# The head of a fused attention block in four chunks instead of two, and a copy of scores moved in front of an exponential in two tiles

## The chip, the cores and the metric

One core of one Trainium2 chip runs the whole program. The metric is the device time of one execution in microseconds (us), and lower is better. The engines are TensorE (PE; its weight loads are shown as PEld), VectorE (DVE), ScalarE (ACT), GpSimd (POOL) and SyncE (SP), which issues all the DMAs of this kernel.

## The reference, cut to what matters

The block has three residual layers: cross-attention over a context of 2048 rows, self-attention with relative positions, and a gated attention layer. Batch is 4, there are 128 queries, the width is 512 and there are 16 heads of 32. The change touches the first layer only:

```python
x = x + cross_attention(layernorm(x), ctx, ctx, Wq, bq, Wk, bk, Wv, bv, Wo, bo)
# in cross_attention
q = (query @ Wq + bq).reshape(Bq, Sq, H, DK)
k = (key @ Wk + bk).reshape(Bq, Sk, H, DK)
v = (value @ Wv + bv).reshape(Bq, Sk, H, DK)
scores = jnp.einsum('bqhd,bkhd->hbqk', q, k) / np.sqrt(DK)
attn = jax.nn.softmax(scores.reshape(H * Bq, Sq, Sk), axis=0)   # over the 64 (head, batch) pairs
out = jnp.einsum('hbqk,bkhd->bqhd', attn, v)
```

The softmax runs over the 64 pairs of head and batch and not over the keys, so each block of 128 keys can be finished by itself.

## The kernel before, in words

**Tiles.** The first layer walks over the context in T = 16 tiles t of 128 keys (times 4 batches, so 512 columns). For each tile TensorE projects the keys K (four banks i, `project_k`, L466) and the values V (four batches b, `project_v`, L489), multiplies queries with keys (four groups of heads w, `score`, L510) and, two tiles later in program order, probabilities with values (`attend`, L533). ScalarE copies K, V and the scores out of PSUM (`k_copy` L1027, `v_copy` L1037, `s_copy` L1045) and takes the exponentials in eight pieces p (`exp`, L1061). VectorE takes the maximum over the 64 pairs (L1540), subtracts it (L1562), sums the exponentials (L1569), inverts (L1582) and scales two pieces of the eight (L1610); GpSimd subtracts it from two pieces (L1378), scales the other six (L1384), and computes the low parts of the context (L1357).

**Two parts.** Each operand of a projection is split into a high part (a rounded copy, by ScalarE or GpSimd) and a low part (a subtraction, by VectorE or GpSimd). Each product has three terms, in the order of `PARTS`: high times high, high data times low weight, low data times high weight.

**Order.** Nothing schedules this program: every engine runs its instructions in the order in which its block of the code issues them, and semaphores (`wait_ge`, `then_inc`) tie the engines. An instruction that waits holds everything behind it on its engine. The SyncE block issues the loads in order; their data goes out on one queue in that order.

**The head.** Before the first tile SyncE loads the first half of the key weight `Wk1` and of the context (512 KB each), the four pieces of x (256 KB each), the second halves, and then `Wq1`, `Wv1` and the small tables. TensorE keeps itself busy with 14 products of the identity (`keep_warm`, L552), and then runs `first_keys(k, n)` for half k and term n (L566), with the transposes of the normalised x (L371) between them, then the queries (`query`, L587), a small product for the relative positions (L607), which waits for `tab_mul`, and the first scores. ScalarE splits the halves (L1069, L1074), takes the square roots of the layer norm (L1004), copies the transposed x (`query_hi`, L1078) and half of the query weight (L1097). VectorE makes the low parts (L1484, L1489), the layer norm (L1457 to L1466), the low part of the transposed x (L1506) and that of the whole query weight (L1509).

**In a tile.** ScalarE's list for tile t begins with k_copy(t, 0), v_copy(t-1, 1) and a context split, then exp(t-1, 0), s_copy(t, 0), exp(t-1, 1), k_copy(t, 1), exp(t-1, 2), v_copy(t-1, 2) and exp(t-1, 3). TensorE waits for these copies in several places. The two that matter here are:

```python
                else:
                    pe.wait_ge(s["s_evac"], min(2 * (C * t + 3 + b) - 1, 2 * C * T))
```

in `project_v` (L486), by which V(t-1, 2) waits for the first of the two copies of s_copy(t, 0), since that bank held those scores; and `pe.wait_ge(s["kv_evac"], k_step(t, w) + 1)` in `score` (L503), by which the scores of group w wait for k_copy(t, w).

## Time and profile before

| | us |
|---|---|
| three runs | 720.54, 720.43, 720.11 |
| median | 720.43 |
| the profiled execution, its own time | 720.23 |
| its span, first to last instruction | 718.4 |
| PE busy in the span | 701.2 (98%) |
| DVE busy | 627.3 (87%) |
| POOL busy | 502.6 (70%) |
| ACT busy | 487.8 (68%) |

A busy share says how full an engine is, not whether it sets the end. For that one follows the chain of waits back from the last instruction, and looks in the timeline at what each engine waited for. The head (up to the first scores) ends at 26.6 us, and the sixteen tiles follow. The granted TensorE clock reads 1.00 in all slices of the span.

### The profile page before, as it was taken

The page shows a single profiled execution, that of the slowest core. Times are in us where ns is not written, and L with a number is a line of the kernel's source. Part 1 is how long each engine was busy: PE and PEld are TensorE (multiplying, and loading weights), DVE is VectorE, ACT ScalarE, POOL GpSimd, SP SyncE. Part 2 cuts the span into 40 slices and gives each one's busy share as a digit, 9 for nine tenths or more (in the row PEclk, how much of TensorE's full clock was granted, in tenths as well). Part 3 has the DMA queues.
Part 4 walks back from the last instruction along what each step waited for, and adds up shares of the span by engine and source line. Part 5 has one row for each costly group of instructions (what it writes and reads, how often), then busy time and mean ns, then how long its engine had stood idle before and what let it go on. Part 6 is the DMA issues. An engine that isn't in the chain of part 4 may idle for free.

```text
span 718.4 us, 17265 instructions
## 1 busy us (share of the span) xinstructions
PE 701.2 (98%) x7511; PEld 561.6 (78%) x7511; DVE 627.3 (87%) x514; ACT 487.8 (68%) x696; POOL 502.6 (70%) x284
## 2 busy tenths in 40 slices
PE   8999999999999999999999999999999999999988
PEld 7777788888888888888888888887668667878876
DVE  6678999999999999999999999999987458977785
ACT  5578668686776867777686776868643446735682
POOL 1564979999999999999999999996894010054400
PEclk9999999999999999999999999999999999999999
DMA  9411020101101010110101011010003899631101
GB/s 332 147 48 34 26 61 2 59 2 59 56 6 61 1 60 1 60 59 2 61 1 61 20 42 60 2 59 2 1 5 113 284 393 385 254 104 59 60 2 58
DMA packets 15675, 55.74 MB, mean 78 GB/s; under 512 B 1648, under 2 KB 2160, under 8 KB 12272
## 3 DMA queue, kind: packets, MB, share of 16 engines
q1 hardware_dynamic: 15600, 54.64, 21.0%
q8 instruction: 59, 0.97, 0.5%
q14 instruction: 16, 0.13, 0.1%
HBM read 43.16 MB, written 11.47 MB: 76 GB/s over the span
## 4 chain that ended last, share of the span: by engine, by line
PE 74%; DVE 12%; DMA 6%; ACT 4%; issue 2%; SPq 1%; POOL 0%; DVEq 0%; POOLq 0%; ACTq 0%
PE ps L466 22%; PE ps L489 21%; PE ps L510 9%; PE ps L533 8%; DMA rel_scratch<-blocks 5%; DVE extra L1540 2%; PE ps L444 2%; PE ps L855 2%; PE ps L380 2%; DVE extra L1569 2%; PE ps L587 2%; PE ps L837 1%; PE ps L388 1%; DVE ps L1569 1%; PE ps L399 1%
## 5 line engine op out<-in xcount | busy, mean ns | idle before, releaser
L1384 POOL TENSOR_TENSOR s_buf<-s_buf,r_all 128x1024 f32<-128x1024 f32 x92 | 195.1, 2159 | 1.0 <-DVE r_all L1582 1.0
L1045 ACT COPY s_buf<-ps 128x1024 f32<-128x1024 f32 x128 | 123.2, 1016 | 30.4 <-PE ps L510 30.4
L1061 ACT ACTIVATE s_buf<-s_buf 128x1024 f32<-128x1024 f32 x128 | 134.2, 1064 | 8.2 <-DVE s_buf L1562 8.2
L1540 DVE TENSOR_REDUCE extra<-s_buf 128x128 f32<-128x2048 f32 x48 | 109.3, 2277 | 4.6 <-ACT s_buf L1045 4.6
L1562 DVE TENSOR_TENSOR s_buf<-s_buf,ps 128x2048 f32<-128x2048 f32 x48 | 106.9, 2282 | 0.5
L1351 POOL TENSOR_TENSOR v_buf<-v_buf,extra 128x512 f32<-128x512 f32 x64 | 81.0, 1301 | 8.2 <-ACT v_buf L1037 8.2
L1037 ACT COPY v_buf<-ps 128x512 f32<-128x512 f32 x64 | 37.6, 587 | 65.2 <-PE ps L489 64.4
L1569 DVE TENSOR_REDUCE ps<-s_buf 128x128 f32<-128x4096 f32 (+1 forms) x16 | 67.6, 4227 | 15.2 <-ACT s_buf L1061 15.1
L1362 POOL TENSOR_TENSOR w_lo<-raw,w_hi 128x2048 fp32r<-128x2048 f32 x5 | 23.1, 4618 | 82.1 <-ACT w_hi L1012 82.1
L510 PEld LDWEIGHTS ps<-q_t,k_t 32*128 32x128 f32 x2048 | 63.0, 186 | 18.9 <-issue 17.5
L510 PE MATMUL ps<-q_t,k_t 32*128 32x128 f32 x2048 | 75.1, 283 | 0.4 <-ACT k_t L1027 0.2
L1569 DVE TENSOR_REDUCE extra<-s_buf 128x128 f32<-128x2048 f32 x32 | 72.8, 2276 | 1.1 <-ACT s_buf L1061 1.1
L1378 POOL TENSOR_TENSOR s_buf<-s_buf,m_all 128x2048 f32<-128x2048 f32 x16 | 66.0, 4124 | 6.9 <-DVE m_all L1555 6.9
L533 PEld LDWEIGHTS ps<-s_buf,v_buf 128*32 128x32 f32 x2048 | 56.3, 108 | 14.7 <-issue 14.3
L533 PE MATMUL ps<-s_buf,v_buf 128*32 128x128 f32 x2048 | 66.0, 278 | 1.3 <-DVE s_buf L1610 1.3
L1357 POOL TENSOR_TENSOR odd_lo<-extra,odd_hi 128x512 fp32r<-128x512 f32 x32 | 41.1, 1300 | 21.9 <-ACT odd_hi L1020 21.8
L1027 ACT ACTIVATE k_t<-ps,cols 128x512 f32<-128x512 f32 x64 | 43.8, 690 | 8.1 <-PE ps L466 3.9
L1357 POOL TENSOR_TENSOR x_lo<-raw,x_hi 128x512 fp32r<-128x512 f32 x28 | 35.9, 1295 | 12.9 <-ACT x_hi L1020 12.7
L1540 DVE TENSOR_REDUCE ps<-s_buf 128x128 f32<-128x2048 f32 x16 | 36.7, 2296 | 6.0 <-ACT s_buf L1045 4.6
L1610 DVE TENSOR_TENSOR s_buf<-s_buf,ps 128x2048 f32<-128x2048 f32 x18 | 41.0, 2285 | 0.5
L1391 POOL TENSOR_TENSOR acc<-acc,late 128x512 f32<-128x512 f32 x26 | 34.0, 1307 | 7.6 <-ACT late L1053 7.6
L466 PE MATMUL ps<-odd_hi,w_hi 128*128 128x512 f32 x128 | 36.3, 405 | 0.0
(265 smaller groups left out, 1476.6 us busy)
## 6 DMA issues: line engine op xcount, KB each, us to landing
rel_scratch<-blocks SPq DMA_DIRECT2D x16, 636.0 KB, 10.8
s_buf<-rel_scratch SPq DMA_DIRECT2D x7, 1210.0 KB, 9.6
extra<-in_ctxT SPq DMA_DIRECT2D x8, 1024.0 KB, 4.9
raw<-in_ctxT SPq DMA_DIRECT2D x7, 1024.0 KB, 4.9
raw<-in_Wq SPq DMA_DIRECT2D x2, 1024.0 KB, 7.2
raw<-in_Wv SPq DMA_DIRECT2D x2, 1024.0 KB, 4.9
extra<-in_EvRel SPq DMA_DIRECT2D x1, 2048.0 KB, 12.5
extra<-rel_scratch SPq DMA_DIRECT2D x1, 1210.0 KB, 10.1
```

Of the source, the lines that this page charges most:

```text
L466: last = mm(ps[:, k_bank(t, i), :], w_parts[v][:, 0, n % C, i * P:(i + 1) * P], ctx_parts[t % 2][u][:, n % C, :], start=n == 0, stop=n == ...
L489: last = mm(ps[:, v_bank(t, b), :], ctx_parts[t % 2][u][:, n % C, b * P:(b + 1) * P], w_parts[v][:, 1, n % C, :], start=n == 0, stop=n == ...
L510: last = mm(pair, k_t[rows, w, keys], q_t[rows, w, keys], start=True, stop=True, skip_group_check=True)
L533: last = mm(ps[j * HD:(j + 1) * HD, bank, b * P:(b + 1) * P], v_of(t)[:, b, h * HD:(h + 1) * HD], probs[:, j, b // 2, :, b % 2], start=b = ...
L1045: copy(piece(t, 2 * w + u).rearrange("p e (u n) -> p (e u) n", u=2), ps[:, 2 * u:2 * u + 2, :]).then_inc(s["s_evac"], 1)
L1061: nc.scalar.activation(piece(t, p), piece(t, p), ACT.Exp).then_inc(s["exp_done"], 1)
L1351: pool.tensor_tensor(v, v, bv_all, ALU.add).then_inc(s["v_ready"], 1)
L1357: pool.tensor_tensor(lo[:, :, rows], raw_of(t)[:, :, rows], hi[:, :, rows], ALU.subtract).then_inc(s["ctx_lo"], 1)
L1384: pool.tensor_tensor(part, part, spread(r_all, 4), ALU.mult).then_inc(s["attn_pool"], 1)
L1540: nc.vector.tensor_reduce(m_ps if k == 0 else m_next[:, k % 2, :], over_pairs(t, 2 * k, 2), AX.XY, ALU.max).then_inc(s["max_done"], 1)
L1562: tt(part, part, m_wide.broadcast_to([P, 8, P, 2]), ALU.subtract).then_inc(s["sub_dve"], 1)
L1569: nc.vector.tensor_reduce(r_ps if k == 0 else z_next[:, k % 2, :], over_pairs(t, p, n), AX.XY, ALU.add).then_inc(s["sum_done"], 1)
```

## The change

SyncE now loads key weight and context in four chunks each (256 KB, one chunk c of 128 rows of the contraction), in turn, and all eight in front of x; the rest follows in the old order. TensorE runs 8 products of the identity instead of 14, and then the keys chunk by chunk with all three terms, only the last term of the last chunk between the transposes. ScalarE and VectorE split chunk by chunk, and the layer norm comes after that. The low part of the query weight is made half by GpSimd and half by VectorE, and VectorE's half comes after the table for the positions; the queries run their terms in the order 0, 2, 1. One copy of K goes between two copies of the transposed x. In tiles 1 and 2 ScalarE runs s_copy(t, 0) and k_copy(t, 1) in front of exp(t-1, 0). The semaphores for the chunks are ones used again later, so that later waits rise by 16.

```diff
+        FIRST_WK = ("wk_in", "wkb_ev_in", "head_rq_in_0", "head_rq_in_1")
+        FIRST_CTX = ("ctx_in_0", "ctxb_b3_in", "head_rq_in_2", "head_rq_in_3")
...
-            first, rest = slice(0, C // 2), slice(C // 2, C)
-            load(wk_raw[:, first], a["Wk1"][:, first], "wk_in")
-            load(raw[:, first], a["ctxT"][0][:, first], "ctx_in_0")
+            for c in range(C):
+                load(wk_raw[:, c], a["Wk1"][:, c], FIRST_WK[c])
+                load(raw[:, c], a["ctxT"][0][:, c], FIRST_CTX[c])
             for b in range(B):
                 load(x_res[:, b, :], a["x"][b], f"x_in_{b}")
-            load(wk_raw[:, rest], a["Wk1"][:, rest], "wkb_ev_in")
-            load(raw[:, rest], a["ctxT"][0][:, rest], "ctxb_b3_in")
...
             pe.wait_ge(s["ident_done"], 2)
-            keep_warm(3, 14)
-            for n in range(3):
-                first_keys(0, n)
+            keep_warm(3, 8)
+            for c in range(C - 1):
+                first_keys(c, range(3))
+            first_keys(C - 1, range(2))
             transposes(y_ln0, 0, 0)
             transposes(y_ln0, 0, 1)
-            first_keys(1, 0)
+            first_keys(C - 1, (2,))
             transposes(y_ln0, 0, 2)
             transposes(y_ln0, 0, 3)
-            first_keys(1, 1)
-            first_keys(1, 2)
             query(0, 0)
+            query(0, 2)
             pe.wait_ge(s["tab_mul"], 1)
...
             query(0, 1)
-            query(0, 2)
...
                 query(w + 1, 0)
                 score(0, w)
+                query(w + 1, 2)
                 query(w + 1, 1)
-                query(w + 1, 2)
...
-            first_weight_hi(0, "wk_in")
-            first_ctx_hi(0, "ctx_in_0")
-            ln_std(0, 0)
-            ln_std(0, 1)
-            first_weight_hi(1, "wkb_ev_in")
-            ln_std(0, 2)
-            first_ctx_hi(1, "ctxb_b3_in")
-            ln_std(0, 3)
+            for c in range(C):
+                first_hi(c)
+            for b in range(B):
+                ln_std(0, b)
             query_hi(0)
-            query_hi(1)
             act.wait_ge(s["wq_in"], 16)
             copy(wq_hi[:, 0:2], wq_raw[:, 0:2]).then_inc(s["wq_split"], 1)
+            query_hi(1)
+            act.wait_ge(s["cols_in"], 16)
+            act.wait_ge(s["ln_done"], B)
+            k_copy(0, 0)
             query_hi(2)
             query_hi(3)
...
-                exp(t - 1, 0)
+                if t > 2:
+                    exp(t - 1, 0)
                 s_copy(t, 0)
 
+                if t <= 2:
+                    k_copy(t, 1)
+                    exp(t - 1, 0)
                 exp(t - 1, 1)
-                k_copy(t, 1)
+                if t > 2:
+                    k_copy(t, 1)
...
             pool.tensor_copy(wq_hi[:, 2:4], wq_raw[:, 2:4]).then_inc(s["wq_split"], 1)
+            pool.wait_ge(s["wq_split"], 2)
+            pool.tensor_tensor(wq_lo[:, 2:4], wq_raw[:, 2:4], wq_hi[:, 2:4], ALU.subtract).then_inc(s["wq_split"], 1)
             pool.wait_ge(s["wv_in"], 16)
...
+            for c in range(C):
+                first_lo(c)
             moments0(0)
...
             normalised(0, 3)
-            first_weight_lo(1)
-            first_ctx_lo(1)
...
-            dve.wait_ge(s["wq_split"], 2)
-            tt(wq_lo[:], wq_raw, wq_hi[:], ALU.subtract).then_inc(s["wq_split"], 1)
             nc.vector.memset(r_all[:], 1.0).then_inc(s["ones_done"], 1)
             dve.wait_ge(s["tab_in"], 16)
...
+            dve.wait_ge(s["wq_split"], 2)
+            tt(wq_lo[:, 0:2], wq_raw[:, 0:2], wq_hi[:, 0:2], ALU.subtract).then_inc(s["wq_split"], 1)
```

The new `first_hi(c)` copies chunk c of the weight and then of the context once each has landed, `first_lo(c)` subtracts both, and `first_keys(c, terms)` runs four products (one per bank) for each term of chunk c.

TensorE at the head, from the keys to the first scores, before (`x_hi`, `x_lo` are the context, `w_hi`, `w_lo` the key weight, `xq` and `wq` the queries' side):

```order
L566 MATMUL ps<-x_hi,w_hi 128x512 x8
L566 MATMUL ps<-x_hi,w_lo 128x512 x8
L566 MATMUL ps<-x_lo,w_hi 128x512 x8
L371 MATMUL ps<-ident,v_buf 128x128 x8
L566 MATMUL ps<-x_hi,w_hi 128x512 x8
L371 MATMUL ps<-ident,v_buf 128x128 x8
L566 MATMUL ps<-x_hi,w_lo 128x512 x8
L566 MATMUL ps<-x_lo,w_hi 128x512 x8
L587 MATMUL ps<-xq_hi,wq_hi 128x512 x4
L607 MATMUL ps<-tab,r_all 128x255
L587 MATMUL ps<-xq_hi,wq_lo 128x512 x4
L587 MATMUL ps<-xq_lo,wq_hi 128x512 x4
```

And now, from the last chunk of the keys on (three chunks of twelve products stand in front of these rows):

```order
L566 MATMUL ps<-x_hi,w_hi 128x512 x4
L566 MATMUL ps<-x_hi,w_lo 128x512 x4
L371 MATMUL ps<-ident,v_buf 128x128 x8
L566 MATMUL ps<-x_lo,w_hi 128x512 x4
L371 MATMUL ps<-ident,v_buf 128x128 x8
L587 MATMUL ps<-xq_hi,wq_hi 128x512 x4
L587 MATMUL ps<-xq_lo,wq_hi 128x512 x4
L607 MATMUL ps<-tab,r_all 128x255
L587 MATMUL ps<-xq_hi,wq_lo 128x512 x4
```

The count of key products is 48 in both, but 44 of them now stand in front of the first transpose, where 24 stood, and the last term of query group 0 is the one with the low weight.

ScalarE between the layer norm's roots and the first copy of queries, before:

```order
L1078 CAST xq_hi<-ps 128x4x128 x2
L1097 CAST wq_hi<-s_buf 128x1024
L1078 CAST xq_hi<-ps 128x4x128 x2
L1027 ACTIVATE k_t<-ps,cols 128x512 x4
L1083 ACTIVATE q_t<-ps,q_add 128x512
```

and now (the line numbers are those of the changed file):

```order
L1073 CAST xq_hi<-ps 128x4x128
L1087 CAST wq_hi<-s_buf 128x1024
L1073 CAST xq_hi<-ps 128x4x128
L1026 ACTIVATE k_t<-ps,cols 128x512
L1073 CAST xq_hi<-ps 128x4x128 x2
L1026 ACTIVATE k_t<-ps,cols 128x512 x3
L1078 ACTIVATE q_t<-ps,q_add 128x512
```

The four copies of the transposed x are spread further, around the copy of the query weight and one of K.

ScalarE in tile 1, before:

```order
L1020 CAST x_hi<-raw 128x4x128
L1061 ACT_TABLE_LOAD
L1061 ACTIVATE s_buf<-s_buf 128x1024
L1045 COPY s_buf<-ps 128x1024 x2
L1061 ACTIVATE s_buf<-s_buf 128x1024
L1027 ACTIVATE k_t<-ps,cols 128x512
L1061 ACTIVATE s_buf<-s_buf 128x1024
L1037 COPY v_buf<-ps 128x512
```

and now:

```order
L1019 CAST x_hi<-raw 128x4x128
L1044 COPY s_buf<-ps 128x1024 x2
L1026 ACTIVATE k_t<-ps,cols 128x512
L1060 ACT_TABLE_LOAD
L1060 ACTIVATE s_buf<-s_buf 128x1024 x3
L1036 COPY v_buf<-ps 128x512
```

The load of the exponential's table and three exponentials now stand behind the copy of K.

## Rows read from the trace of the kernel before

**Rows 1.** The page, busy time of each engine.
```profile
PE 701.2 (98%) x7511; PEld 561.6 (78%) x7511; DVE 627.3 (87%) x514; ACT 487.8 (68%) x696; POOL 502.6 (70%) x284
```

**Rows 2.** Chain of waits, 0 to 100 us: start, length, what.
```profile
56.63 4.43 DVE ps L1569
```

**Rows 3.** Timeline of PE, head: start, length, line, operands, count, idle before.
```profile
8.08 2.08 PE L566 MATMUL ps<-x_hi,w_hi 128*128 128x512 f32 x8 [1.58 <-ACT x_hi L1074]
...
13.62 1.03 PE L371 MATMUL ps<-ident,v_buf 128*128 128x128 f32 x8
...
20.87 1.07 PE L587 MATMUL ps<-xq_hi,wq_hi 128*128 128x512 f32 x4
22.96 0.69 PE L607 MATMUL ps<-tab,r_all 32*128 32x255 f32 x2 [1.02 <-DVE tab L1512]
23.58 1.21 PE L587 MATMUL ps<-xq_hi,wq_lo 128*128 128x512 f32 x4
24.63 1.09 PE L587 MATMUL ps<-xq_lo,wq_hi 128*128 128x512 f32 x4
```

**Rows 4.** Timeline of ACT, head.
```profile
5.01 1.05 ACT L1069 CAST w_hi<-s_buf 128x1024 fp32r<-128x1024 f32 x1 [2.79 <-DMA s_buf<-in_Wk]
...
6.79 1.14 ACT L1074 CAST x_hi<-raw 128x512 fp32r<-128x512 f32 x2 [0.73 <-DMA raw<-in_ctxT]
...
14.26 1.07 ACT L1078 CAST xq_hi<-ps 128x512 fp32r<-128x512 f32 x2 [0.68 <-PE ps L371]
...
15.22 1.06 ACT L1097 CAST wq_hi<-s_buf 128x1024 fp32r<-128x1024 f32 x1
...
25.82 0.69 ACT L1083 ACTIVATE q_t<-ps,q_add 128x512 f32<-128x512 f32 x1 [3.60 <-PE ps L587]
```

**Rows 5.** Timeline of DVE, head.
```profile
8.66 0.69 DVE L1457 BATCH_NORM_STATS2 stats<-x_res 128x6 f32<-128x512 f32 x1
...
13.98 0.55 DVE L1466 TENSOR_SCALAR v_buf<-x_res,mean_var,rstd 128x512 f32<-128x512 f32 x1
...
20.02 2.47 DVE L1509 TENSOR_TENSOR wq_lo<-s_buf,wq_hi 128x2048 fp32r<-128x2048 f32 x1
```

**Rows 6.** Windows of the first 12 us: stretch, busy per engine, PEclk, DMA share, GB/s.
```profile
4.00:6.00 2.00, 2.00 (x17) 2.00 (x16) 0.00 (x0) 0.99 (x1) 0.00 (x0) 1.00 0.97 296
6.00:8.00 2.00, 0.49 (x5) 0.30 (x3) 1.78 (x2) 1.20 (x3) 0.00 (x0) 1.00 1.03 387
```

**Rows 7.** Windows of the identity products alone (L552): PE, PEld, PEclk, DMA share, GB/s.
```profile
3.00:4.00 1.00, 1.00 (x6) 1.00 (x6) 1.00 0.88 254
...
5.00:6.00 1.00, 1.00 (x12) 1.00 (x11) 1.00 0.96 309
```

**Rows 8.** Timeline of ACT, tiles 1 and 3.
```profile
47.87 0.62 ACT L1020 CAST x_hi<-raw 128x512 fp32r<-128x512 f32 x1
48.51 1.28 ACT L1061 ACT_TABLE_LOAD   x1
49.81 1.06 ACT L1061 ACTIVATE s_buf<-s_buf 128x1024 f32<-128x1024 f32 x1
50.78 1.90 ACT L1045 COPY s_buf<-ps 128x1024 f32<-128x1024 f32 x2
...
109.90 1.06 ACT L1061 ACTIVATE s_buf<-s_buf 128x1024 f32<-128x1024 f32 x1 [0.37 <-DVE s_buf L1562]
110.86 1.91 ACT L1045 COPY s_buf<-ps 128x1024 f32<-128x1024 f32 x2
```

**Rows 9.** Timeline of PE, tiles 1 to 3.
```profile
50.33 1.07 PE L466 MATMUL ps<-odd_lo,w_hi 128*128 128x512 f32 x4
...
54.36 1.17 PE L510 MATMUL ps<-q_t,k_t 32*128 32x128 f32 x32 [0.24 <-ACT k_t L1027]
...
81.87 1.20 PE L489 MATMUL ps<-w_hi,odd_hi 128*128 128x512 f32 x4 [1.10 <-ACT s_buf L1045]
...
113.17 1.07 PE L489 MATMUL ps<-w_hi,x_hi 128*128 128x512 f32 x4
```

More of the change, by code:

```diff
@@ L325, in rel_load @@
                 dst = rk_part(u) if kind else rq_part(u)
-                load(dst[:, :, 0:RUN], rows, f"rk_in_{u}" if kind else f"rq_in_{u}")
+                load(dst[:, :, 0:RUN], rows, f"rk_in_{u}" if kind else f"head_rq_in_{u}")
             for n in range(4):
@@ L552, in keep_warm, with first_keys @@
                     mm(ps[:, bank, 0:P], ident[:], ident[:], start=True, stop=True, skip_group_check=True)
-            def first_keys(k, n):
-                u, v = PARTS[n]
-                if n == 0:
-                    pe.wait_ge(s["wkv_hi"], k + 1)
-                    pe.wait_ge(s["ctx_hi"], 2 * k + 2)
-                elif v:
-                    pe.wait_ge(s["wkv_lo"], k + 1)
-                else:
-                    pe.wait_ge(s["ctx_lo"], 2 * k + 2)
-                for hg in range(C):
-                    for c in (2 * k, 2 * k + 1):
+            def first_keys(c, terms):
+                for n in terms:
+                    u, v = PARTS[n]
+                    if n == 0:
+                        pe.wait_ge(s["wkv_hi"], c + 1)
+                        pe.wait_ge(s["ctx_hi"], c + 1)
+                    elif v:
+                        pe.wait_ge(s["wkv_lo"], c + 1)
+                    else:
+                        pe.wait_ge(s["ctx_lo"], c + 1)
+                    for hg in range(C):
                         last = mm(ps[:, k_bank(0, hg), :], w_parts[v][:, 0, c, hg * P:(hg + 1) * P], x_parts[u][:, c, :],
-                                  start=(k, n, c) == (0, 0, 0), stop=(k, n, c) == (1, 2, C - 1), skip_group_check=True)
-                    if (k, n) == (1, 2):
-                        last.then_inc(s["kv_psum"], 1)
+                                  start=(c, n) == (0, 0), stop=(c, n) == (C - 1, 2), skip_group_check=True)
+                        if (c, n) == (C - 1, 2):
+                            last.then_inc(s["kv_psum"], 1)
             def query(hg, n):
@@ L587, in query @@
                     last = mm(ps[:, q_bank(hg), :], (wq_hi, wq_lo)[v][:, c, hg * P:(hg + 1) * P], (xq_hi, xq_lo)[u][:, c, :],
-                              start=n == 0 and c == 0, stop=n == 2 and c == C - 1, skip_group_check=True)
-                if n == 2:
+                              start=n == 0 and c == 0, stop=n == 1 and c == C - 1, skip_group_check=True)
+                if n == 1:
                     last.then_inc(s["q_psum"], 1)
             pe.wait_ge(s["ident_done"], 2)
-            keep_warm(3, 14)
-            for n in range(3):
-                first_keys(0, n)
+            keep_warm(3, 8)
+            for c in range(C - 1):
+                first_keys(c, range(3))
+            first_keys(C - 1, range(2))
             transposes(y_ln0, 0, 0)
             transposes(y_ln0, 0, 1)
-            first_keys(1, 0)
+            first_keys(C - 1, (2,))
             transposes(y_ln0, 0, 2)
             transposes(y_ln0, 0, 3)
-            first_keys(1, 1)
-            first_keys(1, 2)
             query(0, 0)
+            query(0, 2)
             pe.wait_ge(s["tab_mul"], 1)
@@ L1065, in _, with first_hi @@
             act.wait_ge(s["eps_done"], 2)
-            def first_weight_hi(k, name):
-                part = slice(2 * k, 2 * k + 2)
-                act.wait_ge(s[name], 16)
-                copy(w_hi[:, 0, part], wk_raw[:, part]).then_inc(s["wkv_hi"], 1)
-            def first_ctx_hi(k, name):
-                act.wait_ge(s[name], 16)
-                for c in (2 * k, 2 * k + 1):
-                    copy(x_hi[:, c, :], raw[:, c, :]).then_inc(s["ctx_hi"], 1)
+            def first_hi(c):
+                act.wait_ge(s[FIRST_WK[c]], 16)
+                copy(w_hi[:, 0, c], wk_raw[:, c]).then_inc(s["wkv_hi"], 1)
+                act.wait_ge(s[FIRST_CTX[c]], 16)
+                copy(x_hi[:, c, :], raw[:, c, :]).then_inc(s["ctx_hi"], 1)
             def query_hi(b):
@@ L1107, in _ @@
             ctx_split(1, 1)
-            act.wait_ge(s["wkv_lo"], 3)
+            act.wait_ge(s["wkv_lo"], C + 1)
             for w in range(1, C):
@@ L1479, in moments0, with first_lo @@
                 moments(0, b)
-            def first_weight_lo(k):
-                part = slice(2 * k, 2 * k + 2)
-                dve.wait_ge(s["wkv_hi"], k + 1)
-                tt(w_lo[:, 0, part], wk_raw[:, part], w_hi[:, 0, part], ALU.subtract).then_inc(s["wkv_lo"], 1)
-            def first_ctx_lo(k):
-                for c in (2 * k, 2 * k + 1):
-                    dve.wait_ge(s["ctx_hi"], c + 1)
-                    tt(x_lo[:, c, :], raw[:, c, :], x_hi[:, c, :], ALU.subtract).then_inc(s["ctx_lo"], 1)
-            first_weight_lo(0)
-            first_ctx_lo(0)
+            def first_lo(c):
+                dve.wait_ge(s["wkv_hi"], c + 1)
+                tt(w_lo[:, 0, c], wk_raw[:, c], w_hi[:, 0, c], ALU.subtract).then_inc(s["wkv_lo"], 1)
+                dve.wait_ge(s["ctx_hi"], c + 1)
+                tt(x_lo[:, c, :], raw[:, c, :], x_hi[:, c, :], ALU.subtract).then_inc(s["ctx_lo"], 1)
+            for c in range(C):
+                first_lo(c)
             moments0(0)
```

18 lines of the change are left out of this document (8 added, 10 removed).

## The prediction

> **What bounds the kernel now.** I read the page first. TensorE is busy for 701.2 of 718.4 us and VectorE for 627.3 [rows 1], so the kernel is near TensorE's own length, and only time in which TensorE waits, or works on a later schedule than it could, can be won. The chain of waits was next. It begins with the loads and the layer norm, runs along VectorE from 56.63 us [rows 2], and changes to TensorE at 81.87 us, where TensorE had stood 1.10 us for ScalarE's copy of scores [rows 9]. From there to the end of the tiles it stays on TensorE. So there are two limits in turn: VectorE's chain in tiles 0 to 2 and TensorE's from tile 2 on, and a gain must pass through both. The timelines of the head then show where the start is lost: TensorE's first key product at 8.08 us, after 1.58 us without work, and 1.02 us lost at 22.96 us to VectorE's table, which stood behind the 2.47 us subtraction of the whole query weight [rows 3, 5]. All sums below are on the profiled execution, 720.23 us with its 1.8 us around the span; the median of the runs is 0.2 us above it.
>
> **The head, step by step.** Loads: the queue gives its data in order. The first 512 KB were there at 5.01 us, 1 MB at 6.79 us, when ScalarE took them up [rows 4]. The first chunk pair is now exactly the first 512 KB, so ScalarE can copy the context chunk at 5.0 us; one of the two copies of 1.14 us is 0.6 us, and TensorE began 0.15 us after the last one (6.79 + 1.14 = 7.93, then 8.08). First key product: 5.0 + 0.6 + 0.15 = 5.75, I take 5.8 us instead of 8.08. The later pairs come every 1.3 to 1.8 us (512 KB at 387 and at 296 GB/s, [rows 6]) and TensorE needs 2.8 us for each, so only the first pair counts.
>
> TensorE: 24 key products took 13.62 - 8.08 = 5.54 us, 0.23 each [rows 3]. Now 44 stand in front of the transposes: 5.8 + 44 x 0.23 = 15.9 us. The layer norm took 13.98 + 0.55 - 8.66 = 5.9 us of VectorE [rows 5]; it now comes after the last low part of a context chunk (2 MB at 9.7 us by the rates above, two copies and subtractions behind it: 11.1 us) and ends at 17.0 us, its second quarter near 15. TensorE asks for the second quarter at 16.3 and for the last at 17.7, so moving it costs nothing, with 0.7 us of cover.
>
> ScalarE becomes the bound here. Its first copy of transposed x began 0.64 us after the transposes (14.26 against 13.62, [rows 3, 4]): 16.55 us. Then come, less the overlap of neighbours, 0.5 (x), 1.0 (query weight, 1.06 in the row), 0.5 (x), 0.6 (one K copy, priced by the same form at 25.82 us), 0.5 and the last 0.6 [rows 4]: 20.2 us. Query group 0 can start at 20.35 us, 0.5 us earlier than its 20.87, while TensorE waits some 1.9 us. But then little is lost: 0.92 for the first term, 0.92 for the second, which needs the low part of x (VectorE, 20.8 us, in time), the product for positions at 22.2 (its table is now in front of the weight's subtraction and ready at 21.3), 0.62 to the last term at 22.8 us, which needs both halves of the low weight. GpSimd's half is done near 20.4 (from 18.05, at twice VectorE's length at most 2.5); VectorE's takes half of 2.47 and ends at 22.55, so 0.25 us of cover. Before, the last group began at 24.63 and the copy of queries at 25.82, 1.19 later, and a group behind the product for positions is 0.13 longer (1.05 against 0.92): the copy starts at 24.1 us. **Head: 25.82 - 24.1 = -1.7 us.** The value weight's low part (the form of 2.47 us, behind the product for positions) ends near 25.7 us, and the first scores (0.7 for the copy, 1.2 for the products) near 26.0, so it stays hidden. What follows up to tile 1 is TensorE without a wait and moves as a block.
>
> **Tile 1, ScalarE** (times in the old frame, to be moved by the head). The context split ends at 48.49. Before, table load, exponential, scores copy and K copy followed without a gap [rows 8]. Now the scores copy runs 48.51 to 50.41 and the K copy waits for its product, which ends at 50.33 + 1.07 = 51.40 [rows 9]. So ScalarE stands 1.0 us, and the table load, which starts only when the copy has ended, and all that is behind it come later by 1.0 plus some 0.2 of overlap lost: the fourth exponential by 1.25 us. VectorE's sum at 56.63 waits for it and begins the chain [rows 2], so **VectorE's chain is 1.25 us later**. In return TensorE's 0.24 us at 54.36 and, in tile 2, the 1.10 us at 81.87 go [rows 9], because the scores copy no longer stands behind an exponential; about 0.8 us come back as waits for ScalarE's later K copy and GpSimd's later scaled pieces. TensorE enters tile 3 some 0.6 us ahead.
>
> **Tile 3** keeps the old order. There the exponential at 109.90 waits for VectorE, and the scores copy at 110.86 is behind it; TensorE took the bank at 113.17 [rows 8, 9]. With VectorE's chain 1.25 us late the exponential starts at 111.15, the copy at 112.1, its first half ends at 113.1, and TensorE goes on at 113.15 with 0.13 us for a restart, although it was ready at 112.6. The stall removed in tile 2 is back in tile 3. **Tiles: +0.1 us** against before. From then on VectorE, with 627 us of work against TensorE's 701 [rows 1], makes its lateness up, and the order no longer matters.
>
> **Sum:** 720.23 - 1.7 + 0.1 = **718.6 us**. What is not in the trace: the cost of 2 KB rows for the first chunks. The bounds for the first pair are 5.0 us, when as many bytes were there before, and 6.8 us, when twice as many were [rows 4]; earlier than 5.0 it can't be, as ScalarE stood waiting for those bytes. I take 5.0, since the bytes and their place in the queue are the same; the upper end would eat the whole 1.7. The Trainium skill ("DMA: Bandwidth & Descriptors", Measured) speaks against it: it wants at least 1 MiB in a DMA for 75% of peak and gives 138 GB/s for 64 KB and 341 for 1 MB. At an estimated 250 GB/s by that page the pairs would come every 2.1 us, still under TensorE's 2.8 us, and the sum would lose only what the first pair is late.
>
> **The rivals.**
> (a) *Both stalls go.* If ScalarE's standing in tile 1 is smaller than I count, VectorE is not late and TensorE keeps its 0.6 us: 720.23 - 1.7 - 0.6 = 717.9. The waits in rows 8 and 9 speak against it.
> (b) *Chunks land or are served late.* The first pair 0.6 us late, or one of the thin covers (0.25 us for the low weight, 0.7 for the layer norm) broken: 1 us of the 1.7 lost, 719.6. For it: the first megabyte came at 296 GB/s, later ones at 387 [rows 6].
> (c) *The clock.* The granted clock reads 1.00 throughout, but of the identity products only 6 are seen between 3 and 4 us and 12 between 5 and 6 [rows 7], so TensorE worked at the lower of its two levels (1.2 GHz) until near 4.9 us and at 2.4 GHz after. The 28 records ended at 6.49; 16 now end at about 5.1, hardly past that point, and a gap of 0.7 us follows. If the raise does not come, key products take 0.43 instead of 0.23 us: 0.2 us each. With 8 of them low the head's gain is gone (720.2), with 16 the kernel is slower by 1.6 us, with 24 (two chunks) by 3.2: 723.4. It decides from the ninth product on. Against it: 1.58 us without work in front of the first key product did not lower the clock before. The Trainium skill ("TensorE: Matmul & The Clock Gate", What's actually happening) says that activity releases a throttled default, and at no fixed point of the kernel; by that rule the shorter warming could miss the raise in some runs, and the sum would be that of 8 to 24 low products.
> (d) *No change:* the head's gain ends in a wait on another engine before tile 1, 720.2.
>
> **Numbers.** Forecast 0.56 (own range 717.9 to 719.3), (a) 0.12, (b) 0.17, (c) 0.09, (d) 0.06. A measurement of this kernel tells 0.2% (1.44 us) from no change. Against the median of 720.43 that is 718.99: four fifths of the forecast's chance and (a) lie below, 0.56 in all; slower by over 0.2% is most of (c), 0.07; the rest, 0.37, is the same. The range leaves out the far ends of (a) and (c): 717.5 to 720.3.
>
> **What would show it.** First key product at 5.8 us, and key products at 0.23 us from the first on (else (c)); transposes at 15.9; a wait of some 1.9 us of TensorE for ScalarE in front of the queries; copy of queries at 24.1; in tile 1 1.0 us of idle ScalarE in front of the K copy and the table load behind it; no wait at tile 2's value product, and one of about 0.5 us at tile 3's. The prediction is wrong if the chain of waits stays on TensorE from tile 1 on, or if the first key product is later than 6.5 us.

## The result and the profile after

The changed kernel takes 722.54 us (median of 11 executions, 721.37 to 723.45), the kernel before 720.51 us beside it (11, 720.11 to 720.90). The ratio is 1.0029, with a 95% interval of 1.0021 to 1.0036: **slower by some 2 us**, where I had forecast 718.6. It is also more scattered: 2.1 us from the fastest to the slowest, where the kernel before has 0.8.

The profiled execution took 722.82 us, its span is 721.0. TensorE's timeline of the head comes first (start, length, line, operands, count, idle before). These rows answer to [rows 3].

```profile
1.52 3.42 PE L552 MATMUL ps<-ident 128*128 128x128 f32 x16 [1.52 <-POOL ident L1333]
6.89 1.25 PE L566 MATMUL ps<-x_hi,w_hi 128*128 128x512 f32 x4 [1.95 <-ACT x_hi L1069]
7.94 1.91 PE L566 MATMUL ps<-x_hi,w_lo 128*128 128x512 f32 x4
9.64 1.83 PE L566 MATMUL ps<-x_lo,w_hi 128*128 128x512 f32 x4
11.31 1.09 PE L566 MATMUL ps<-x_hi,w_hi 128*128 128x512 f32 x4
...
18.61 1.03 PE L371 MATMUL ps<-ident,v_buf 128*128 128x128 f32 x8
...
22.88 1.19 PE L587 MATMUL ps<-xq_hi,wq_hi 128*128 128x512 f32 x4 [1.43 <-ACT xq_hi L1073]
23.91 1.08 PE L587 MATMUL ps<-xq_lo,wq_hi 128*128 128x512 f32 x4
25.39 0.69 PE L607 MATMUL ps<-tab,r_all 32*128 32x255 f32 x2 [0.40 <-DVE tab L1503]
26.52 1.21 PE L587 MATMUL ps<-xq_hi,wq_lo 128*128 128x512 f32 x4 [0.44 <-DVE wq_lo L1506]
```

The first key product starts at 6.89 us, earlier than the 8.08 before but 1.1 us later than forecast. Then eight products take 11.31 - 7.94 = 3.37 us, 0.42 each, against 0.23 for those behind them. The windows of the same stretch (busy time per engine, then PEclk, DMA share, GB/s) name the reason:

```profile
4.00:6.00 2.00, 0.94 (x7) 0.75 (x5) 0.69 (x1) 0.51 (x1) 0.00 (x0) 1.00 0.82 166
6.00:8.00 2.00, 1.11 (x5) 0.92 (x6) 0.89 (x2) 1.38 (x3) 0.00 (x0) 0.96 1.00 355
8.00:10.00 2.00, 2.00 (x6) 1.58 (x5) 1.98 (x4) 1.70 (x3) 0.00 (x0) 0.50 1.01 326
10.00:12.00 2.00, 2.00 (x7) 1.55 (x6) 1.20 (x3) 1.24 (x2) 0.00 (x0) 0.69 1.07 409
```

TensorE ran at its lower level (1.2 GHz) from 7.8 to 11.2 us, after a wait of 1.95 us behind the short warming. The GB/s column shows 166 where it showed 296 [rows 6]. ScalarE took the first context chunk at 6.13 us:

```profile
6.13 0.62 ACT L1069 CAST x_hi<-raw 128x512 fp32r<-128x512 f32 x1 [1.62 <-DMA raw<-in_ctxT]
...
27.83 0.69 ACT L1078 ACTIVATE q_t<-ps,q_add 128x512 f32<-128x512 f32 x1 [3.26 <-PE ps L587]
```

The copy of queries is at 27.83 us, 2.0 later than before [rows 4] and 3.7 later than forecast. The third place is VectorE and GpSimd near 23 us:

```profile
23.71 1.62 DVE L1503 TENSOR_TENSOR tab<-tab 32x255 f32<-32x255 f32 x1
25.26 1.21 DVE L1506 TENSOR_TENSOR wq_lo<-s_buf,wq_hi 128x1024 fp32r<-128x1024 f32 x1
...
20.86 2.36 POOL L1341 TENSOR_TENSOR wq_lo<-s_buf,wq_hi 128x1024 fp32r<-128x1024 f32 x1 [3.19 <-ACT wq_hi L1087]
23.16 1.90 POOL L1344 CAST w_hi<-s_buf 128x2048 fp32r<-128x2048 f32 x1
```

The product of the tables took 1.62 us; before it took 0.35, so that the subtraction behind it and the last query term are late. In this execution the head's 3.7 us against the forecast are then landing 1.1, clock 1.6 (8 x 0.2) and VectorE's late table 1.0.

The tiles cost what was forecast, though not quite in the way that was forecast. ScalarE in tile 1 and, below, in tile 3 (these answer to [rows 8]), and TensorE's new waits and its value product of tile 3 ([rows 9]):

```profile
50.55 1.93 ACT L1044 COPY s_buf<-ps 128x1024 f32<-128x1024 f32 x2
53.47 0.69 ACT L1026 ACTIVATE k_t<-ps,cols 128x512 f32<-128x512 f32 x1 [0.98 <-PE ps L466]
54.18 1.28 ACT L1060 ACT_TABLE_LOAD   x1
...
113.00 1.06 ACT L1060 ACTIVATE s_buf<-s_buf 128x1024 f32<-128x1024 f32 x1 [1.71 <-DVE s_buf L1555]
113.97 1.91 ACT L1044 COPY s_buf<-ps 128x1024 f32<-128x1024 f32 x2
```

```profile
63.35 1.17 PE L510 MATMUL ps<-q_t,k_t 32*128 32x128 f32 x32 [0.43 <-ACT k_t L1026]
87.59 1.17 PE L510 MATMUL ps<-q_t,k_t 32*128 32x128 f32 x32 [0.56 <-ACT v_buf L1036]
...
115.02 1.19 PE L489 MATMUL ps<-w_hi,x_hi 128*128 128x512 f32 x4
```

ScalarE stands 0.98 us in front of the K copy, the table load is behind it, and in tile 3 the value product comes 1.85 us later than at 113.17. The scores behind it start at 118.98 against 116.89 us: 2.09 late, where the copy of queries was 2.01 late. So the tiles cost 0.08 us. But the wait of about 0.5 us that I had put at the value product of tile 3 is not there: that row starts 0.1 us late at most. TensorE gives back what it had won in smaller pieces, most of it earlier: 0.43 us in tile 1 for a copy of K and 0.56 us in tile 2 for a copy of V. The last scores (505.08 before, 507.22 now) keep this distance.

Another 0.45 us appears between 600 and 628 us in the second layer. There TensorE waits for a load from `rel_scratch` (the relative positions' terms, written to memory and read back), 0.69 us before and 1.09 us now:

```profile
613.18 1.97 PE L746 MATMUL ps<-ident,s_buf 128*128 128x128 f32 x16 [0.69 <-DMA s_buf<-rel_scratch]
```

```profile
615.72 1.97 PE L745 MATMUL ps<-ident,s_buf 128*128 128x128 f32 x16 [1.09 <-DMA s_buf<-rel_scratch]
```

This wait differs between executions of one kernel. In the other profiles the same stretch takes between 0.1 us less and 1.0 us more than in the kernel before, and the changed kernel alone has 0.45, 0.03 (e9) and 0.97 (e13, where VectorE waits for such a load). What makes these loads late was not looked into.

### The profile page after: what moved, and what is told of

The parts are those of the page before. It is cut to its first block, busy times and chain, and to the rows that moved or that the text cites. A ratio compares the mean times of both kernels' runs of the same rounds, so it can differ in the third digit from the quotient of the medians.

```text
span 721.0 us, 17252 instructions
## 1 busy us (share of the span) xinstructions
PE 701.8 (97%) x7499; PEld 561.3 (78%) x7499; DVE 627.5 (87%) x516; ACT 488.6 (68%) x698; POOL 504.6 (70%) x285
## 4 chain that ended last, share of the span: by engine, by line
PE 78%; DVE 8%; DMA 6%; ACT 5%; issue 2%; SPq 1%; POOL 0%; DVEq 0%; POOLq 0%
PE ps L466 23%; PE ps L489 21%; PE ps L510 9%; PE ps L533 8%; DMA rel_scratch<-blocks 4%; PE ps L566 2%; PE ps L444 2%; PE ps L854 2%; PE ps L380 2%; ACT s_buf L1060 2%; PE ps L587 1%; PE ps L836 1%; PE ps L388 1%; PE ps L399 1%; DVE extra L1562 1%
```

## The experiments

All were compared with the kernel before on their own chip, where its median was 720.45 to 720.69 us. Medians differ somewhat from session to session: the changed kernel itself gave 722.54, 722.40 (e9) and 721.99 (e13), so a difference of up to half a microsecond between two sessions says little by itself.

**e1: the warming undone.**

```diff
-            keep_warm(3, 8)
+            keep_warm(3, 14)
```

> The changed kernel with 14 products of the identity again instead of 8. Theory (clock): in the changed kernel TensorE started the keys at 6.89 us after 1.95 us without work, and the granted clock read 0.50 from 7.8 to 11.2 us, so 8 key products took 0.43 us instead of 0.23, about 1.6 us. With 14 the identity products end near 6.5 us, the gap in front of the keys is under 1 us, the granted clock stays at 1.00, and the transposes begin near 17.0 instead of 18.61 us: about 720.9 us, 1.6 below the changed kernel. Rival (the low clock came from the slow landing of the chunks or costs nothing, because ScalarE's chain bounds the head): clock or not, the copy of queries still starts near 27.8 us, and the time stays at 722.5.

721.62 us, ratio 1.0017 (1.0008 to 1.0026): 0.9 of the 1.6 expected. This is between theory and rival. The key products are all at 0.23 us, but now the low level comes later:

```profile
21.40 1.71 PE L587 MATMUL ps<-xq_hi,wq_hi 128*128 128x512 f32 x4 [1.80 <-ACT xq_hi L1073]
22.91 1.91 PE L587 MATMUL ps<-xq_lo,wq_hi 128*128 128x512 f32 x4
```

```profile
20.00:22.00 2.00, 0.60 (x2) 0.51 (x3) 1.63 (x3) 2.00 (x5) 2.00 (x2) 0.96 1.01 402
22.00:24.00 2.00, 2.00 (x6) 1.55 (x5) 2.00 (x4) 1.10 (x2) 1.58 (x1) 0.50 1.08 372
```

The wait of 1.80 us in front of the queries, which the change also makes, was followed by products at the lower level. Of its 11 executions six had a mean granted clock of 0.998 or less (722.5 us on average), five had 1.00 (721.1).

**e2: GpSimd's copy of the value weight behind the low query weight.**

```diff
             pool.wait_ge(s["wkv_hi"], C)
+            pool.wait_ge(s["wq_split"], 4)
             pool.tensor_copy(w_hi[:, 1], wv_raw).then_inc(s["wkv_hi"], 1)
```

> The changed kernel, in which GpSimd's copy of the value weight waits until both halves of the low query weight are done. Theory (contention of GpSimd and VectorE): VectorE's product of the tables took 1.62 us beside GpSimd's subtraction and copy where it took 0.35 before; here at least the second half of that cover is gone, the product of positions and the last query term come up to 1.0 us earlier, the copy of queries starts near 26.8 instead of 27.83 us: 721.5 us. As the subtraction of 2.36 us is still beside VectorE, half of it may remain: up to 722.0. Rival (the table's load landed late, or VectorE waits for something else): the product of the tables stays at 1.6 us, and with the value weight now later the kernel gets slower, 722.5 to 723.5.

721.68 us, ratio 1.0010 (1.0000 to 1.0020): 0.9 us below the changed kernel and inside the expected range. The table is fast again, 0.5 us after GpSimd's subtraction had ended:

```profile
19.03 2.36 POOL L1341 TENSOR_TENSOR wq_lo<-s_buf,wq_hi 128x1024 fp32r<-128x1024 f32 x1 [1.37 <-ACT wq_hi L1087]
23.52 1.90 POOL L1345 CAST w_hi<-s_buf 128x2048 fp32r<-128x2048 f32 x1 [2.13 <-DVE wq_lo L1507]
```

```profile
20.53 1.29 DVE L1500 TENSOR_TENSOR xq_lo<-ps,xq_hi 128x512 fp32r<-128x512 f32 x2 [0.37 <-ACT xq_hi L1073]
...
21.88 0.35 DVE L1504 TENSOR_TENSOR tab<-tab 32x255 f32<-32x255 f32 x1
```

This execution happened to have a full clock and an early first chunk, so it shows the head without late landing, low clock and late table: keys at 5.93 us, transposes at 16.02, copy of queries at 25.02. That is 0.8 us less than before and 0.9 more than the forecast of 24.1. The rest is in ScalarE's rows:

```profile
17.23 0.29 ACT L1003 ACTIVATE rstd<-mean_var,gtmp 128x1 f32<-128x1 f32 x1 [1.15 <-DVE mean_var L1459]
17.43 0.57 ACT L1073 CAST xq_hi<-ps 128x512 fp32r<-128x512 f32 x1
```

ScalarE takes all four square roots in front of its first copy of transposed x, and the fourth waits for VectorE's statistics until 17.23 us. The copy starts at 17.43 and not at 16.55, and the queries at 21.04 and not at 20.35. The remaining 0.2 us lie in the query products behind them (2.05 us to the product of positions, where I had 1.84).

But the lead of 0.8 us is given back at once, since the held copy now comes too late for the value weight's low part, and that for ScalarE's first copy of scores:

```profile
25.52 2.29 DVE L1514 TENSOR_TENSOR w_lo<-s_buf,w_hi 128x2048 fp32r<-128x2048 f32 x1 [1.28 <-POOL w_hi L1345]
```

```profile
27.85 1.93 ACT L1044 COPY s_buf<-ps 128x1024 f32<-128x1024 f32 x2 [1.11 <-DVE w_lo L1514]
```

In e5 (below), with the table late and the copy of queries at 25.88, this copy of scores starts at 27.93. So e2 shows what made the table late, but its 0.9 us of time are not shown to come from that.

**e3 and e4: the order of the tiles on the old head**, in tiles 1 and 2, and in tile 2 alone.

```diff
-                exp(t - 1, 0)
+                if not (t == 2):
+                    exp(t - 1, 0)
                 s_copy(t, 0)
+                if t == 2:
+                    k_copy(t, 1)
+                    exp(t - 1, 0)
                 exp(t - 1, 1)
-                k_copy(t, 1)
+                if not (t == 2):
+                    k_copy(t, 1)
```

(e4; in e3 the condition is `t <= 2`.)

> The kernel before, with only the new order of ScalarE in tiles 1 and 2 (copy of scores and of K in front of the first exponential). Theory (as in the prediction): the stalls of 0.24 and 1.10 us go, ScalarE stands 1.0 us in tile 1 in front of the K copy, VectorE's chain is 1.25 us late, and the stall comes back in tile 3: +0.1 us, between 720.2 and 720.9 us for 720.5 before. Rival (the tiles' part alone gives the 2 us by which the changed kernel is slower, or gives its 1.3 us of stalls): 722.5, or 719.2.

> The kernel before, with the new order of ScalarE in tile 2 alone. Theory: it is the table load behind the K copy in tile 1 that makes VectorE late; without tile 1's reordering ScalarE's exponentials of tile 0 keep their place, TensorE's 1.10 us at the value product of tile 2 goes, and the exponentials of tile 1 are late by the copies only (3 us at most on ScalarE, which has slack): 719.4 us if nothing comes back, up to 720.0 if the later exponentials hold VectorE. Rival (TensorE can't get ahead, because VectorE's chain bounds it in tile 3 anyway): the stall is found again in tile 3, and the time stays at 720.5.

e3: 720.56 us beside 720.69, ratio 1.0002 (0.9993 to 1.0010). e4: 719.55 us, ratio 0.9988 (0.9979 to 0.9997). Both as the theory has it. The exponential of tile 3 tells them apart, e3 first:

```profile
110.95 1.06 ACT L1061 ACTIVATE s_buf<-s_buf 128x1024 f32<-128x1024 f32 x1 [1.77 <-DVE s_buf L1567]
```

```profile
109.82 1.06 ACT L1061 ACTIVATE s_buf<-s_buf 128x1024 f32<-128x1024 f32 x1 [1.08 <-DVE s_buf L1567]
```

Before it was at 109.90 [rows 8]. The order in tile 1 makes VectorE 1.1 us late and takes back what tile 2's order gives. In e4, too, TensorE waits 0.56 us for a copy of V, at 85.01, which I had not seen: there remain 0.86 us, from the copy of queries (25.88) to the scores of tile 3 (116.09) 90.21 us, against 91.07 before.

**e5: the changed head with the old tiles.**

> The changed kernel with the old order of ScalarE in tiles 1 and 2, so the head's changes alone. Theory: the head carries all of the loss; with the tiles worth 0.0 (measured alone: 720.56 beside 720.69) this gives the changed kernel's time, 722.3 to 722.8 us, and TensorE stands 0.24 and about 1.1 us in tiles 1 and 2 again. Rival (the new order of the tiles only hurts on top of the late head): 721.0 to 721.5.

721.47 us, ratio 1.0012 (1.0003 to 1.0021), less than expected and inside the rival's range. In its profile (720.44 us) the head has a full clock and the first chunk at 5.45 us, the table takes 1.62 us, and the copy of queries is at 25.88, where it is in the kernel before (25.82). So with roots and table alone nothing is left of the forecast gain of 1.7, and nothing is lost either; the head's loss needs the low clock or a late chunk. Whether the new tile order costs 1 us on this head stayed open until e13 and e14.

**e6 and e7: both cures; and the value weight shared.** e6 is e1 with e2. In e7 the value weight is copied half by ScalarE, in its wait in front of the queries' copy, and half by GpSimd:

```diff
+            act.wait_ge(s["wv_in"], 16)
+            copy(w_hi[:, 1, 0:2], wv_raw[:, 0:2]).then_inc(s["wkv_hi"], 1)
             act.wait_ge(s["qadd_done"], 1)
             query_copy(0)
...
+            pool.wait_ge(s["wq_split"], 4)
-            pool.tensor_copy(w_hi[:, 1], wv_raw).then_inc(s["wkv_hi"], 1)
+            pool.tensor_copy(w_hi[:, 1, 2:4], wv_raw[:, 2:4]).then_inc(s["wkv_hi"], 1)
```

> The changed kernel with 14 products of the identity and with GpSimd's copy of the value weight behind the low query weight, the two cures together. Each alone took about 0.9 to 1.1 us from the changed kernel. Theory (two separate causes): they add up, 720.5 to 720.8 us. Rival (both cured the same thing, the clock, which fell in some executions): no more than one of them alone, 721.6.

> As the kernel with both cures, but ScalarE, idle for 3.8 us in front of the copy of queries, copies half of the value weight, and GpSimd's half is 1.0 instead of 1.9 us. Theory: the low value weight comes about 1.0 us earlier, ScalarE no longer waits 1.1 us for it in front of the first copy of scores, and the 0.52 us that TensorE stood at the scores of group 1 go: 0.5 us below the kernel with both cures, 720.0 to 720.3. Rival (the copy on ScalarE holds the copy of queries, or the 0.52 us are hidden later): the same as the kernel with both cures.

721.99 us, ratio 1.0020 (1.0010 to 1.0030), and 721.64 us, 1.0013 (1.0003 to 1.0023). Both miss: the cures don't add, and e6 has e2's late value weight as well. Again six of 11 executions each had a mean clock of 0.998 or less. Those averaged 722.7 and 722.3 us, the other five 721.1 and 720.4. The profile of e6 fell among the former, with the low products where e1 had them:

```profile
21.13 1.19 PE L587 MATMUL ps<-xq_hi,wq_hi 128*128 128x512 f32 x4 [1.74 <-ACT xq_hi L1073]
22.17 1.86 PE L587 MATMUL ps<-xq_lo,wq_hi 128*128 128x512 f32 x4
23.95 1.21 PE L607 MATMUL ps<-tab,r_all 32*128 32x255 f32 x2
25.10 2.08 PE L587 MATMUL ps<-xq_hi,wq_lo 128*128 128x512 f32 x4
```

**e8, e10 and e11: TensorE's wait in front of the queries filled.**

```diff
+            pe.wait_ge(s["xq_split"], 1)
+            keep_warm(0, 5)
             query(0, 0)
```

e10 is the changed kernel with this and 14 products in front; e11 has e7's sharing of the value weight too; e8 is e11 with the new order in tile 2 alone.

> As the kernel with the split value weight, with five products of the identity in TensorE's wait of 1.7 us in front of the queries (so that the granted clock does not fall there, as it did at 21.9 us with 14 products in front), and the new order of ScalarE in tile 2 alone. Theory: the tile part gives 1.1 us as it did alone, the filled gap some 0.3 us on average (1.3 us in the executions in which the clock fell): 718.6 to 719.0 us, the first version that beats both kernels. Rival (the early head reaches VectorE's chain and gives nothing behind it): the same 719.6 as the old head with tile 2's order.

> The changed kernel with 14 products of the identity at the start and five more in TensorE's wait in front of the queries, nothing else. Theory (clock): with the front alone 6 of 11 executions showed a mean granted clock of 0.998 or less and took 722.5 us, the other five 721.1; with the wait filled no execution shows less than 0.999, and the median is 721.1, with GpSimd's contention still in it. Rival (the low clock comes at random, whatever TensorE does in the head): clocks of 0.998 in four to six executions of 11, and 721.6 us or more.

> The kernel with all cures of the head (14 and five products of the identity, value weight split), but the changed kernel's order in tiles 1 and 2. Against the one with the new order in tile 2 alone, 719.75 us, it tells what the order in tile 1 costs on a steady head. Theory (the table load behind the K copy makes VectorE 1.25 us late and the stall comes back in tile 3): 1.0 to 1.2 us more, 720.8 us, and TensorE waits or is held at tile 3's value product. Rival: 719.75, as tile 1's own stall of 0.24 us goes.

e10: 721.40 us, ratio 1.0009 (1.0000 to 1.0018). e11: 720.76 us, 0.9998 (0.9989 to 1.0007). e8: 719.75 us, 0.9987 (0.9978 to 0.9996). e10 and e11 are near their theory; e8 misses it (718.6 to 719.0) and lies at its rival. In none of these 33 executions was the mean clock below 0.999, where 18 of 33 were at or below 0.998 with the wait left open (e1, e6, e7); on one chip it was none of 11 (e8) beside six of 11 (e7). So the low level there comes with the wait. The table product in e10 (GpSimd's copy first) shows the contention with everything else in order:

```profile
21.76 1.89 POOL L1346 CAST w_hi<-s_buf 128x2048 fp32r<-128x2048 f32 x1
```

```profile
22.30 1.63 DVE L1505 TENSOR_TENSOR tab<-tab 32x255 f32<-32x255 f32 x1
```

The steps from e10 to e11 to e8 give 0.6 us for the value weight (one chip) and 1.0 us for tile 1's order (across chips; e3 and e4, on one chip, give the same).

**e9, e13 and e14: the changed kernel twice more, and its head with the old tiles on the same chip as e13.**

> The changed kernel itself once more, on the same chip as the next three. With the old order of the tiles the same head took 721.47 us on another chip, 1.1 less than the changed kernel's 722.54, though the new order alone cost nothing on the old head. Theory (the executions differ by when the first chunks land and by the clock, and chips too): 721.5 to 722.6 us, and a new profile in which the first context chunk lands at another time than 6.11 us. Rival (the new order of the tiles costs 1.1 us when the head is late): 722.5 again.

> The changed kernel a third time, beside its head alone on the same chip. Theory (its executions differ by the point at which the clock is raised, which the profiles show at 4.4 and at 10.7 us): a median from 721.4 to 722.6, and within 0.4 us of the head alone. Rival (the new order of the tiles costs 1.0 us on this head): 1.0 us above the head alone.

> The changed head with the old order of the tiles, beside the changed kernel on the same chip. Theory: within 0.4 us of it, since from the copy of queries at 25.88 us to the scores at 116.96 us its profile showed 91.08 us and the changed kernel's 91.15. Rival: 1.0 us below it.

e9: 722.40 us, ratio 1.0012 (0.9998 to 1.0025), from 9 executions of which one took 719.95; so its interval takes in no change; theory and rival both allowed this median. e13: 721.99 us, ratio 1.0020 (1.0011 to 1.0030); e14: 721.69 us, 1.0014 (1.0005 to 1.0023). On one chip 0.3 us lie between new and old tiles, as in the theory. Each interval is some 0.7 us to either side, so these times alone do not exclude the rival of 1.0 us; the profiles do. From the copy of queries to the scores of tile 3 they have 91.15 us with the new order (e13, and the changed kernel's first profile) and 91.06 and 91.08 with the old one (e14, e5), which makes 0.1 us. The profile of e9 shows where an execution can lose without the first chunk being late (it was taken up at 5.07 us):

```profile
5.83 2.05 PE L566 MATMUL ps<-x_hi,w_hi 128*128 128x512 f32 x4 [0.53 <-ACT x_hi L1069]
7.68 1.91 PE L566 MATMUL ps<-x_hi,w_lo 128*128 128x512 f32 x4
9.38 1.71 PE L566 MATMUL ps<-x_lo,w_hi 128*128 128x512 f32 x4
10.94 1.09 PE L566 MATMUL ps<-x_hi,w_hi 128*128 128x512 f32 x4
```

Nearly twelve key products are at the low level, since here the higher one came only at 10.7 us. The PEclk column reads 1.00 in this stretch, so the lengths of the products have to tell it. Those of e13 and e14 (2.05 us for the first four) say the same, up to 9.7 and 9.6 us.

**e15: the cured head with the old tiles.**

> The head with all cures and the old order of the tiles. Beside the same head with the changed kernel's order (720.76 us) and with tile 2 alone (719.75). Theory: 720.4 to 720.9 us, as the old order costs what the changed one costs. Rival (the changed order costs 1.0 us on a new head): 719.7.

720.25 us, ratio 0.9995 (0.9986 to 1.0004), 0.15 us below the theory's range. On this head the changed order is 0.5 us above the old one (e11, the same chip in an earlier session), not 1.0. In the two profiles the stretch to tile 3 differs by 0.06 us alone (25.67 to 116.80 and 25.82 to 116.89).

**e12 and e16: the old head with the table in front**, with and without tile 2's order.

```diff
-            dve.wait_ge(s["wq_split"], 2)
-            tt(wq_lo[:], wq_raw, wq_hi[:], ALU.subtract).then_inc(s["wq_split"], 1)
             nc.vector.memset(r_all[:], 1.0).then_inc(s["ones_done"], 1)
             dve.wait_ge(s["tab_in"], 16)
             tt(pos_w[0:HD, 0:2 * P - 1], tab[0:HD, 1, 0:2 * P - 1], tab[0:HD, 2, 0:2 * P - 1],
                ALU.mult).then_inc(s["tab_mul"], 1)
+            dve.wait_ge(s["wq_split"], 2)
+            tt(wq_lo[:], wq_raw, wq_hi[:], ALU.subtract).then_inc(s["wq_split"], 1)
...
             query(0, 0)
+            query(0, 2)
             pe.wait_ge(s["tab_mul"], 1)
...
             query(0, 1)
-            query(0, 2)
```

> The kernel before with three of the change's steps only: VectorE's product of the tables in front of the subtraction of the query weight, the query terms in the order 0, 2, 1 with the product of positions between the last two, and the new order of ScalarE in tile 2. The loads, the two halves and the 14 products of the identity stay. Theory: TensorE's 1.02 us in front of the product of positions go, the copy of queries comes at 24.8 instead of 25.82 us, and with the 1.1 us of tile 2 this gives 718.5 us, below both kernels and below tile 2's order alone (719.55). Rival (GpSimd's copy of the value weight, which runs to 20.3 us, now holds the product of the tables, or VectorE's later chain takes the lead back): 719.5.

> The kernel before with VectorE's product of the tables in front and the query terms in the order 0, 2, 1, without the tile part. Theory: the two parts of the best version add up. It has 1.0 us from the head (copy of queries at 24.85 instead of 25.82) and 0.86 from tile 2: here 719.6 to 719.8 us. Rival (the early head is waited away in tile 1 or 2 if the old order stays): 720.4.

e12: 718.93 us, ratio 0.9973 (0.9963 to 0.9983), the best version and below both kernels, though 0.4 above its theory. e16: 719.68 us, 0.9989 (0.9980 to 0.9998), as expected. Within the intervals the two parts add up: 1.1 us (e4) and 1.0 (e16) against 1.8 together. TensorE in e12 has no wait left in front of the product of positions:

```profile
21.03 1.07 PE L587 MATMUL ps<-xq_hi,wq_hi 128*128 128x512 f32 x4
21.94 1.07 PE L587 MATMUL ps<-xq_lo,wq_hi 128*128 128x512 f32 x4
22.93 0.69 PE L608 MATMUL ps<-tab,r_all 32*128 32x255 f32 x2
23.56 1.20 PE L587 MATMUL ps<-xq_hi,wq_lo 128*128 128x512 f32 x4
```

## Why the prediction was wrong, step by step

The tiles' term held. In the head's term of -1.7 us three steps failed, each of which had stood at no cost: key products at the full clock from the first on (1.0 to 1.6 us lost in e14, e13 and e9), the low weight inside its cover (1.0 us lost) and the layer norm moved for nothing (0.7 us lost).

**The first pair of chunks at 5.0 us: right within 0.1 to 0.6 us.** In the profiled execution it was 6.13 us, but in the twelve other profiles with these loads ScalarE took the chunk up between 5.07 and 5.64 us. 6.13 was the exception, and this execution's first key product at 6.89 us is past the 6.5 that I had named as a sign of being wrong. The 166 GB/s between 4 and 6 us hardly moved the first pair, and the later ones never held TensorE.

**Key products at 0.23 us from the first on: failed, and the largest single part in the profiled execution (1.6 of 3.7 us).** I chose against rival (c) because 1.58 us without work had not lowered the clock before. But before, the keys begin at 8.08 us, behind any raise of that kernel's profiles (the latest at 7.4 us, in e3). The changed kernel's keys begin near 6 us. Of the six profiles with 8 products in front, four had 8 to 12 key products at the low level: three because the raise came at 9.6 to 10.7 us, one because the level fell again at 7.8 us after the wait. With 14 products in front none of the twelve others did, new or old head. So rival (c)'s mechanism was at work, and at 0.09 it was far too unlikely; I took the raise near 4.9 us of one trace for a property of the kernel. But (c) alone does not give the time: by its own price eight low products only use up the gain (720.2). The measured loss needed rival (b) as well, whose thin cover for the low weight broke, and no rival had both. The Trainium skill ("TensorE: Matmul & The Clock Gate", What's actually happening) calls the number of slow products variable from run to run; the profiles agree, with 0 (e2, e5), 8 and nearly 12 for one head.

**A wait of 1.9 us in front of the queries at no cost: not safe.** The wait came as forecast (1.4 to 1.8 us). I had priced it as time alone, but it can lower the level too: with 14 products in front this happened in about half of the executions. Whether it cost the changed kernel anything is not shown: in the six profiles with 8 products the level held there. Both clock places together are worth 1.0 us on the median (e10 against e9; 0.6 against e13).

**The low weight's cover of 0.25 us: failed.** I put GpSimd's subtraction and the copy of the value weight beside VectorE's table and subtraction and counted each by its own length. The table product, 0.35 us, took 1.62 because it ended only when GpSimd's copy had. Cost: 1.0 us between the queries and their copy (4.94 us in e5, whose queries began 0.1 us earlier, and 3.98 in e2), and 0.6 us on the median (e10 to e11).

**The layer norm moved at no cost: failed by 0.7 us,** where the keys are in time. The transposes were covered as I said (16.02 us), but I left out that `query_hi(0)` stands behind all four roots on ScalarE: the first copy was 0.9 us late and the queries 0.7 (e2). This is read from the rows; no experiment moved the roots. With the 0.2 us in the query products the head's best case is 0.8 us (e2) and not 1.7.

**Tiles +0.1: right in size, in part by luck.** 0.08 us in the profile and no difference in e3. ScalarE's wait of 1.0 us, the table load behind the K copy, VectorE's lateness and the absence of a wait at tile 2's value product are in the rows. But the forecast had 0.8 us come back in tiles 1 and 2 and 0.5 us at tile 3's value product; it was about 1.1 us in the former (0.43 for K, 0.56 for V and smaller ones) and 0.1 at that product, the rest in small delays behind it. Tile 1's order is what spoils tile 2's 0.86 us (e3 against e4).

**The sum again,** by the start of the copy of queries in the profiles:

| | copy of queries, us |
|---|---|
| forecast | 24.1 |
| roots, and 0.2 in the query products (e2) | 25.02 |
| and the late table (e5); before, 25.82 | 25.88 |
| and 8 to 12 low key products (e14, e13, e9) | 26.92, 26.98, 27.44 |
| 8 low ones and the late first chunk (the changed kernel's first profile) | 27.83 |

The head is thus 2.8 to 3.7 us later than forecast where the clock is low, and 1.8 where it is full. 718.6 and these give 720.4 us with a full clock (e5's profile: 720.44) and 721.4 to 722.3 with a low one; the wait for `rel_scratch` adds up to 1.0 us in some executions. For the profiled one it is 718.6 + 3.7 + 0.45, or 722.8 against 722.82 measured. The medians, 722.5, 722.4 and 722.0, lie in that range. How often an execution has which of these is not known beyond the profiles, so the medians are not split exactly. The clock's 1.0 us on the median is itself a lower bound, as 14 products delay the keys to 6.3 to 7.5 us.

## What to carry to other kernels

Work moved forward to the start of a kernel can land where TensorE's clock has not risen for good (here the rise came between 4.4 and 10.7 us); leave warming long enough to meet the work, and read the level from the lengths of products in several executions, not from one. A wait of nearly 2 us on TensorE can cost more than itself, and a few idle products in it made the kernel steadier (executions from 720.6 to 722.2 us in e10, from 720.5 to 723.8 in e1). Before work is given to GpSimd, look which of VectorE's instructions with two operands in SBUF stand beside it, and a cure that only delays GpSimd's work can cost elsewhere what it gives (e2). Ask of every instruction on an engine what stands in front of it in program order: four short roots held the first copy here; and try the cheap half of a change alone (here a reordering of two VectorE instructions and one tile): it held all of the gain.

## What the runs showed of the hardware

- VectorE's product of the tables (both operands in SBUF, 0.35 us by itself) took 1.62 us where it began soon after GpSimd's copy of the value weight. It ended 0.27 to 0.3 us after that copy did: 25.33 and 25.06 us in the changed kernel, 23.93 and 23.65 in e10. VectorE's subtractions of xq_lo, with one operand in PSUM, were not held: two took 1.29 us at 20.53 in e2, the first of them beside GpSimd's subtraction, and in the kernel before four took 2.47 us from 17.63, beside GpSimd's copy of the value weight (18.45 to 20.35). The Trainium skill ("GPSIMD Engine Reference", Specifications) says that GpSimd shares its SBUF interfaces with VectorE and contends with instructions that have two SBUF inputs; the profiles agree, and show that the short instruction lasted until the long one had ended.
- The higher clock level came at 4.4 us in one profile and at 10.7 us in another of the same kernel (8 products in front). With 14 products, in twelve profiles, it came between 4.8 and 7.5 us.
- The first context chunk, 256 KB behind 256 KB, came between 5.07 and 6.13 us (thirteen profiles).
